# Layer 2's probabilities turned by a transposing DMA instead of TensorE, and four of the weight splits between the layers moved

## What is computed

```
# layer 1: 12 heads of 64; tanh scores, softmax over the neighbours, elu, a gate
feat = elu(softmax(mask(leaky(src + dst'))) @ h + b)
x    = layernorm(x + gate * feat + (1 - gate) * x)
# layer 2: 6 heads of 128
q, k, v = x @ Wq + bq, x @ Wk + bk, x @ Wv + bv
probs   = softmax(q @ k' / sqrt(128) + bias(adj))      # 64 x 64 for each graph and head
x       = layernorm(x + (probs @ v) @ Wf + bf)
```

## Time and profile before

| | us |
|---|---|
| median of 3 runs | 2761.08 (2758.80 to 2764.57) |
| the profiled execution | 2758.91 |
| its span on the core | 2757.2 |
| PE busy | 2725.7 (99% of the span) |
| DVE, ACT, POOL busy | 1678.7, 1212.6, 929.3 |
| layer 2 from group 1 on, one group | 56.1 |

### The profile page before, as it was taken

One profiled execution on the slowest core, in us unless ns is written; L12 is line 12 of the kernel. 1 busy time (PEld: TensorE's weight loads), 2 busy tenths in 40 slices (PEclk: granted clock), 3 DMA queues, 4 the chain that ended last, 5 costly groups with the idle time before them and its releaser, 6 DMA issues.

```text
span 2757.2 us, 51888 instructions
## 1 busy us (share of the span) xinstructions
PE 2725.7 (99%) x20988; PEld 2518.9 (91%) x20988; DVE 1678.7 (61%) x3334; ACT 1212.6 (44%) x3109; POOL 929.3 (34%) x566
## 2 busy tenths in 40 slices
PE   8999999999999989999999999999999999999998
PEld 6877878787888889999999999999999999999998
DVE  6899998888888665454445444444545444444543
ACT  5666676666666633333332333323333333333332
POOL 2453434434344122423333233323333333323330
PEclk9999999999999999999999999999999999999999
DMA  5655665555555521222222222322222222222220
GB/s 180 172 136 143 172 159 138 140 138 143 139 139 140 172 72 59 72 71 80 69 62 77 81 70 59 81 71 80 59 70 70 81 70 60 80 81 70 58 70 24
DMA packets 306895, 269.50 MB, mean 98 GB/s; under 512 B 227808, under 2 KB 244192, under 8 KB 306656
## 3 DMA queue, kind: packets, MB, share of 16 engines
q1 hardware_dynamic: 306656, 266.19, 35.4%
HBM read 142.65 MB, written 75.89 MB: 79 GB/s over the span
## 4 chain that ended last, share of the span: by engine, by line
PE 84%; DVE 6%; DMA 4%; issue 2%; ACT 2%; SPq 1%; POOL 0%; DVEq 0%; ACTq 0%; POOLq 0%
PE ps_hg L1052 18%; PE ps_k L70 15%; PE ps_a L1226 15%; PE ps_a L70 14%; PE ps_q L70 14%; DMA dst_all<-dst_scratch 2%; PE ps_s L1167 2%; PE ps_c L1192 2%; DMA dst_scratch<-dst 1%; ACT logits L563 1%; PE ps_pv L1084 1%; PE ps_pt L1192 1%; PE ps_t L1071 1%; DVE logits L788 1%; DVE dst L805 1%
## 5 line engine op out<-in xcount | busy, mean ns | idle before, releaser
L1052 PE MATMUL ps_hg<-w_hi,xT 128*128 128x512 f32 x2268 | 745.6, 401 | 5.9 <-DVE h_one L821 5.9
L1052 PEld LDWEIGHTS ps_hg<-w_hi,xT 128*128 128x128 f32 x2268 | 426.2, 188 | 109.3 <-issue 7.9
L1052 PE MATMUL ps_hg<-w_lo,xT 128*128 128x512 f32 x1134 | 448.4, 395 | 0.0
L70 PE MATMUL ps_k<-x1T_hi,wk_hi 128*128 128x256 f32 x1152 | 329.0, 286 | 0.0
L70 PE MATMUL ps_k<-x1T_lo,wk_hi 128*128 128x256 f32 x1152 | 321.8, 279 | 0.0
L70 PE MATMUL ps_k<-x1T_hi,wk_lo 128*128 128x256 f32 x1152 | 321.1, 279 | 0.0
L70 PE MATMUL ps_q<-x1T_hi,wq_hi 128*128 128x256 f32 x1140 | 319.3, 280 | 0.0
L70 PE MATMUL ps_q<-x1T_lo,wq_hi 128*128 128x256 f32 x1140 | 318.5, 279 | 0.0
L70 PE MATMUL ps_q<-x1T_hi,wq_lo 128*128 128x256 f32 x1140 | 317.8, 279 | 0.0
L654 ACT ACTIVATE qT<-ps_q,bq_col 128x256 f32<-128x256 f32 x192 | 80.7, 471 | 461.3 <-PE ps_q L70 461.3
L495 POOL TENSOR_TENSOR th_src<-th,wsrc_all 128x768 f32<-128x768 f32 x64 | 118.3, 1849 | 480.1 <-DVE dst_all L801 459.4
(11 more groups left out here) (150 smaller groups left out, 5759.1 us busy)
## 6 DMA issues: line engine op xcount, KB each, us to landing
x_tok<-x SPq DMA_DIRECT2D x64, 384.0 KB, 4.1
dst_all<-dst_scratch SPq DMA_DIRECT2D x128, 192.0 KB, 3.4
gate_scratch<-gate SPq DMA_DIRECT2D x64, 384.0 KB, 2.6
feat_scratch<-feat SPq DMA_DIRECT2D x128, 192.0 KB, 2.8
feat_in<-feat_scratch SPq DMA_DIRECT2D x62, 384.0 KB, 3.1
gate_in<-gate_scratch SPq DMA_DIRECT2D x62, 384.0 KB, 3.7
x_even<-x SPq DMA_DIRECT2D x16, 768.0 KB, 4.2
x_odd<-x SPq DMA_DIRECT2D x16, 768.0 KB, 4.4
```

Of the source, the lines that this page charges most:

```text
L70: ins = pe.matmul(out, left[a][c], right[b][c], start=(n == 0), stop=(n == len(terms) - 1))
L1052: ins = pe.matmul(ps_hg[:, cols], left[a][c], right[b][c], start=(c == 0 and n == 0), stop=(c == KC - 1 and n == 2))
```

## The change

From group 2 on, PE transposes no probabilities. POOL splits `scores_sb` into two planes of 16 bits (`split_p1`), SP issues one transposing DMA of four 128x128 blocks for each pair (`turn_p1`), and ACT and DVE join the planes while they copy the blocks to the diagonal (`join_block` in place of `copy_block`). Of pairs 0 and 1 ACT and DVE join one tile each; of pair 2 ACT joins both. There is one buffer of planes on either side: the DMA of a pair waits until the pair before has been joined, and POOL's split waits until the DMA before has landed. `logits_of` waits for POOL's split where it waited for PE's transposes, `scores` waits for `logit_done` of the pair before. On ACT the join of pair 1 stands behind the second value copy; on DVE it stands behind `logits_of(G, 2)`, and both halves of the input's rsqrt are ahead of `normalise(G, 2)`. Groups 0 and 1 keep the transposes on PE.

At the edge, `Wv`'s chunks 3 to 5 are split ahead of `k_out(0, 1)` on ACT and right behind `normalise(0, 0)` on DVE; `Wf`'s chunks 0 to 2 are rounded ahead of `exps(0, 1)`, 3 to 5 ahead of the first value copy; DVE takes the rests right behind `normalise(0, 1)` and `normalise(0, 2)`. `elu` of the last tile stands ahead of `mix(1, 1)`. SP loads `bf_all` ahead of the last store of features.

```diff
+        def join_block(copy, buf, t, g, signal):
+            s = graph(g)
+            out_ = probs1T[s, buf, :, s].bitcast(U16).rearrange("p (h t) (n l) -> p l h t n", t=GT, l=2)[:, :, :, t, :]
+            copy(out_, planes_p1T[t * NODES:(t + 1) * NODES, :, :, s]).then_inc(signal, 1)
...
+            def turn_p1(G, j):
+                sp.wait_ge(split_p1_done, pair_of(G, j))
+                for joined_ in (block0_done, block1_done):
+                    sp.wait_ge(joined_, 2 * (PAIRS * G + j))
+                sp.dma_start_transpose(planes_p1T.rearrange("p l h n -> p (l h) n"),
+                                       planes_p1.rearrange("p l (h m) -> p (l h) m", h=2)).then_inc(turned_p1, 16)
...
                     sp.wait_ge(mixed, GT * (G + 2) + 1)
                     feat_and_gate(G + 2, 1)
+                if BY_DMA <= G + 1 < NG:
+                    for j in range(PAIRS):
+                        turn_p1(G + 1, j)
...
+            def split_p1(G, j):
+                pool.wait_ge(probs_done, PAIRS * G + j + 1)
+                if pair_of(G, j) > 1:
+                    pool.wait_ge(turned_p1, 16 * (pair_of(G, j) - 1))
+                pool.tensor_copy(planes_p1[:, :, :], scores_sb.rearrange("p k m -> p (k m)").bitcast(U16)
+                                 .rearrange("p (d l) -> p l d", l=2)).then_inc(split_p1_done, 1)
...
-                if 1 <= G < NG - 1:
-                    for t in range(GT):
+                for t in range(GT):
+                    if 1 <= G < NG - 1:
                         feat_less_x(G + 1, t, feat_in[:, :])
                         times_gate(G + 1, t, feat_in[:, :], gate_in[:, :])
+                    if G >= BY_DMA:
+                        split_p1(G, t)
+                if G >= BY_DMA:
+                    split_p1(G, GT)
...
+                    act.wait_ge(turned_p1, 16 * pair_of(G, j))
+                    for g in range(2):
+                        join_block(act.copy, (G + j) % 2, 0, g, block0_done)
+                    if j == PAIRS - 1:
+                        for g in range(2):
+                            join_block(act.copy, (G + j) % 2, 1, g, block1_done)
...
                 else:
-                    dve.wait_ge(pt1_done, PAIRS * G + j)
+                    dve.wait_ge(split_p1_done, pair_of(G, j - 1))
...
             def scores(G, j):
+                if G >= BY_DMA:
+                    pe.wait_ge(logit_done, PAIRS * G + j)
...
-                transpose_probs1(G, 0)
+                if G < BY_DMA:
+                    transpose_probs1(G, 0)
...
             store_feat(NT - 2)
+            sp.wait_ge(gate_stored, 16 * NT)
+            sp.wait_ge(att_done, NT)
+            sp.dma_start(bf_all[:, :], bf.partition_broadcast(P)).then_inc(bf_in, 16)
             store_feat(NT - 1)
```

More of the change, by code:

```diff
@@ L720, in _ @@
                     gate_of(NT - 1)
+                    for n in range(3, KC):
+                        w1_round(act, EARLY_W1 + n)
                 k_out(G, 1)
@@ L723, in _ @@
                     elu_exp(NT - 2)
-                    for n in range(3, KC):
-                        w1_round(act, EARLY_W1 + n)
                 q_out(G, 2)
@@ L731, in _ @@
                 probs_out(G, 0)
+                if G == 0:
+                    for n in range(KC, KC + 3):
+                        w1_round(act, EARLY_W1 + n)
                 exps(G, 1)
                 if G == 0:
+                    elu_exp(NT - 1)
                     whole_gate(1, 1, gate_in[:, :])
@@ L736, in _ @@
                 if G == 0:
-                    elu_exp(NT - 1)
-                    for n in range(KC, KC + 3):
+                    for n in range(KC + 3, 2 * KC):
                         w1_round(act, EARLY_W1 + n)
@@ L742, in _ @@
                 value_out(G, 0)
[L743 removed]
+                if G < BY_DMA:
+                    probs_out(G, 1)
                 exps(G, 2)
                 value_out(G, 1)
+                if G >= BY_DMA:
+                    probs_out(G, 1)
                 value_out(G, 2)
                 if G == 0:
[L748 to L749 removed]
                     act.wait_ge(feat_stored, 32 * NT)
@@ L977, in _ @@
                 normalise(G, 0)
+                if G == 0:
+                    for n in range(3, KC):
+                        w1_rest(dve, EARLY_W1 + n)
+                    elu(NT - 2)
+                    attention(NT - 1)
                 if G + 1 < NG:
@@ L980, in _ @@
                 if G == 0:
-                    elu(NT - 2)
-                    attention(NT - 1)
-                    for n in range(3, KC):
-                        w1_rest(dve, EARLY_W1 + n)
                     dve.wait_ge(bd_zero, 1)
```

78 lines of the change are left out of this document (50 added, 28 removed).

## The result

| | before | after |
|---|---|---|
| median of the timed runs | 2761.08 us (2758.8 to 2764.57) | 2774.47 us (2773.74 to 2779.79) |
| ratio, 95% interval | | 1.0059 (1.0048 to 1.0069) |
| span of the profiled execution | 2757.2 us | 2772.7 us |
| mean granted clock | 0.996 | 0.994 |

The change made the kernel 13.4 us, 0.6%, slower. I had predicted 2735 us, with 2725 to 2748 as the range, and gave slower 0.08.

What follows compares the result with a forecast made beforehand. PE, busy 99% of the span, was taken to bound the kernel. 20.4 us from its transposes plus 6 us at the edge made 26.4 us off, a median of 2735 us, range 2725 to 2748.

Steps and rivals of the forecast that it cites:

- slower: Rival: pair 2's landing stays at 5.7 us, PE waits 1.5 us in each of 30 groups, net 2780 us; chance 0.08.
- the deadline of pair 0: In each group, planes turn by 2041.5 to 2042, DVE's joins take 0.8 us, logits move about half a microsecond at most.
- PE's transposes: In 30 groups, removing them from PE saves 0.68 us each, priced by starts: 20.4 us (18.0 to 21.3).
- The other pieces of the chain: Per pair: POOL's split 0.6 us (at most 1.7), DMA landing 2.8 (2.4 to 5.7), one join 0.38 (0.26 to 0.51).
- Deadline of pair 2: In each group, pair 2's blocks are joined at 2060.4, PE reads them about 2061.9 at the earliest: some 1.1 us slack.
- a late third pair: Small rival: DMA some 5 us, joins 0.5; PE waits up to 0.7 us a group, 9 us back, 2744 us; chance 0.15.
- The edge: Between the layers, PE's waits of 4.4 and 4.1 us and slow clock, less new waits: 6 us gained, bounds 3 and 13.5.
- The two waits that I walked to: At the edge, PE waits 2 us for `k_out(0, 2)` before scores and 1.5 to 4 us before `first_context`.

Runs made afterwards that it cites:

- logits first: The kernel after, with DVE's logits of pair 1 moved ahead of its two joins of pair 0 from group 2 on: 2742.52 us, ratio 0.9942.
- load later: The kernel after, with SyncE issuing pair 0's transfer of planes ahead of the feature and gate load: 2740.08 us, ratio 0.9937.
- edge only: The kernel after with the DMA path switched off, PE transposing in every group, so only the edge's orders remain: 2756.59 us, ratio 0.9994 to before.
- reduction kernels: The kernel after, with DVE's joins written as reductions over a one-element axis instead of copies, ACT's joins staying copies: 2741.44 us, ratio 0.9939.
- POOL waits: The kernel after, with one added wait so that POOL's additions start only when DVE has joined pair 0: 2745.60 us, ratio 0.9957.

## Why the prediction was wrong, step by step

- **The step that failed** is the deadline of pair 0: "DVE's joins (0.8 us) stand ahead of their logits, so these move by about half a microsecond at most". The place was right, and so was the landing (2041.5 to 2042 forecast, 4.1 to 4.6 us behind the gate load's issue; 4.4 us in the group shown; in 11 of the 29 groups it was later than forecast, by up to 1.7 us). The joins' size was wrong: 3.4 us in place of 0.8. Alone a join on DVE takes 0.31 us, within my bounds. But these bounds of 0.26 and 0.51 us came from a copy on ACT out of PSUM and said nothing on what a DVE copy within SBUF does beside POOL. I had even written that the gate load lands at 2041.1, just ahead of the planes, and POOL's additions hang on that load. I didn't put the two sentences together.
- I cited the rule and used it in the wrong place. The Trainium skill (SBUF — State Buffer, SBUF: two separate sides) says that a DVE instruction in a 2-port perf mode, or with two SBUF inputs, and one of POOL exclude each other for a whole instruction, and that ACT never waits. I applied its second case to the `Wf` rests at the edge, where three chunks in 7.62 us beside POOL bear it out, and not its first case to the joins. What the runs show fits the page: joins that end 0.2 us behind a POOL instruction, ACT's untouched, the reductions untouched. Which mode each instruction is in stands in no row.
- **My range left the slow case to the wrong rival.** "Slower" hung on the landing of pair 2's planes. That was 2.4 us in all groups but two and 2.9 at most (forecast 2.8, bounds 2.4 to 5.7), so that rival was rightly small. A rival "DVE's joins beside POOL's additions", 3.4 us in place of 0.8 in 29 groups, less the slack, should have stood there: two additions of 1.85 us are the bound from the trace. That the total came out at 2774, near that rival's 2780, is chance; the mechanism is another.
- **PE's transposes: right.** 20.4 forecast, 19.1 measured when they were added and 20.1 by PE's busy time without them, inside 18.0 to 21.3. Pricing by starts and not by length held.
- **The other pieces of the chain.** ACT's join 0.48 us (0.38 forecast, bound 0.51): four in a row took 2.0, not 1.5, and leave little slack. POOL's split 1.10 us in the mean (0.6 forecast): alone it takes 0.60, as at 1929.14, but 1.27 (the median) when it starts 0.15 us behind DVE's addition, which fits the same exclusion from the other side:

```profile
2057.57 0.95 DVE L908 SCALAR_TENSOR_TENSOR x_even<-x_even,feat_in 128x768 f32<-128x768 f32 x1
...
2057.72 1.27 POOL L550 COPY planes_p<-scores_sb 128x512 uint16<-128x512 uint16 x1 [3.29 <-DVE scores_sb L998]
```

- **Deadline of pair 2**: I called it the only near one. In the kernels without the long waits it has 3 to 6 waits left, 2 to 6 us in all: about the size of the small rival "a late third pair" (9 us), but not for the reason it gave. Pair 2's own planes land after 2.4 us, 2.9 at most. It is pair 0's planes that were late there: in logits first the five waits stand in just the five groups where these took 5.2 to 6.4 us, and everything behind them in the group is late. In load later pair 0's planes are early and four short waits remain; in the first of these groups ACT's list was held 2.2 us by the gate load, which now lands last. In after the 10.0 us come mostly from the late logits.
- **The edge**: 6 us forecast, 2.2 measured with the edge alone (at most 4.1), 3.8 by the first logits of group 2 in the two profiles (1079.62 before, 1075.83 after). Of these 3.8, 1.5 had come about before the edge began: group 0's first normalisation stands at 954.85 before and at 953.35 after. Counted from there it is 2.3 us, and 1.4 in the profile of edge only (956.05, 1079.38). PE's first value started at 964.5, ahead of the 966 that I had named, and the outputs at 993.8, 1.5 us ahead of before and just past my 987 to 993. The two waits that I walked to came, but longer (3.6 and 4.0 us; forecast 2 and 1.5 to 4), and with them the loss of clock (0.57 in the 4 us behind the first, 0.50 behind the second).

The sum as the runs leave it: 19.1 from PE, 2.2 from the edge, 2 to 6 lost to late third pairs, is 15 to 19 us faster, and the load-later and reduction kernels are 18.8 and 17.5 us faster. The forecast of 26.4 was thus some 8 us too high, of which the edge is 4, the third pair 2 or more, the transposes 1; both kernels would lie within my range. The remaining 34 us, which turn the sign, are the joins beside POOL: 23 in waits and some 12 in PE's busy time, most of it by the clock. DVE's joins were busy 81 us longer in after than in POOL waits (118.8, 37.6); less than half of that reached the end.

## What to carry to other kernels

When a copy moves to DVE with both sides in SBUF, look up what POOL does at that moment, not how long the copy is alone: here each of the two copies lasted until 0.2 us behind a POOL addition of 1.85 us. The two were set off by neighbouring entries of one DMA queue and met in 29 of 30 groups, so such a meeting isn't an accident that averages out. The cure can be very small: another place in the order, the copy on ACT, or another DVE instruction for the same bytes. And a median over all transfers of a line hides a step that is late each time: take the landing by its place in the iteration.

## What the runs showed of the hardware that I had not expected

- A DVE copy of 16-bit numbers within SBUF, 256 on 64 partitions, takes 0.31 us alone and up to 2.0 us beside POOL's additions of 1.85 us; a DVE reduction that moves the same bytes takes 0.45 us in both cases, ACT's copy 0.48 in both.
- The transposing DMA of four blocks lands 2.4 us after its issue in the median, the one of twelve blocks 4.0. The issue of the four takes 1.19 us.
- That median hides pair 0's transfer. It is issued directly behind the gate load, and in after it took 3.6 to 5.8 us to land in each of the 29 groups that have such a load, 2.4 in the one that has none; pair 2's took 2.4 to 2.9. Ahead of the gate load (load later) pair 0's took 2.4 us in 28 of 30 groups, 4.0 at most. That fits two transfers in each other's way. The longest of all was 5.6 to 6.4 us in the kernels with the gate load first and 4.1 to 4.6 in those with the planes first; why some groups are worse than others stays open.
- Of the five stalls of 2.1 to 3.1 us ahead of scores in the groups of after, four were followed by 4 us at a granted clock of 0.50 to 0.59 and one (2.1 us, at 1659.6) by none below 1.00. Behind those of 0.9 to 1.1 us, and behind each of the 18 of up to 0.8 us ahead of the contexts, the clock was 1.00 over the next 4 us.
